# Cross-attention with layer norm: where the scale step runs, how the last keys are packed, and the order of all queues

## The chip, the cores and the metric

The kernel runs on one core of a Trainium2 chip. The time is the device time of one execution in microseconds (us); lower is better. TensorE (PE in the rows) multiplies into PSUM, VectorE (DVE), ScalarE (ACT) and GpSimd (POOL) compute elementwise, and the sync engine (SP) issues the transfers. Each engine takes its instructions in program order and waits on semaphores set by the others.

## What is computed

```python
qh = split_heads(q @ Wq.T + bq)     # q: x, 4 x 2048 x 512, 16 heads of 32
kh = split_heads(k @ Wk.T + bk)     # k, v: ctx, 4 x 77 x 512
vh = split_heads(v @ Wv.T + bv)
scores = einsum("bhqd,bhkd->bhqk", qh, kh) / sqrt(32)
scores = where(mask == 0, -1e9, scores)
m = max(scores, axis=-1, keepdims=True)
e = exp(scores - m) * mask
probs = e / (sum(e, axis=-1, keepdims=True) + 1e-9)
attn = einsum("bhqk,bhkd->bhqd", probs, vh)
x = attn @ Wo.T + bo + q
return (x - mean(x)) / sqrt(var(x) + 1e-5) * ln_g + ln_b
```

All in float32; the mask is all ones. There are 8192 query rows and 77 keys for each of 4 batches.

## The kernel before

The rows are cut into 16 blocks b of 512; four blocks belong to a batch. A matrix product of full width is done with operands split in a high and a low part (three products into one PSUM bank). For a block the steps are:

- XH and XL (ScalarE, GpSimd) split the transposed x into `xT_hi` and `xT_lo`; Q(b, c) on TensorE gives 128 of the 512 columns of the query, c = 0 to 3, in bank `proj`; QE (ScalarE) adds the bias and moves it to `QT`.
- S_round(b, j), j = 0 to 2, computes the scores of one block of 32 keys for all 16 heads: 16 small matmuls with `ident` bring in the mask as a bias, 16 more multiply `KT` by `QT`, each on a 32 x 32 tile of the array, into the four banks `ring`. The order of key blocks is `KBLOCK` = 2, 0, 1. TI (VectorE) transposes two banks at a time from `ring` into `E`, so queries lie on partitions. `E` holds 80 columns for each head and row group of a query tile, 77 of them keys.
- MX(b, h) reduces E to the row minimum (scores have a minus sign) for one half of the query groups, h = 0, 1. EX(b, h, r) are 8 exponentials on ScalarE over 77 keys each, with the row's minimum as the bias and the sum accumulated; r = 0 to 3 are the heads of a column block; these 8 are called a group below, and two of them, (h, r) and (h, r + 1), a unit. EPS adds 1e-9, RC (VectorE) inverts, NM (GpSimd, line 643) multiplies a unit by it.
- TO (VectorE) transposes back into `PT_main` (two key blocks) and `PT_tail` (the last keys, of heads r and r + 1 in the two halves of one 32 block). AV(b, h) multiplies by `V_main` and `V_tail` into `ring`, 48 matmuls of 32 x 32 tiles. Two instructions make one float32 matmul, so the rows count 96.
- AH and AL (ScalarE, VectorE) split the result, OUT(b, t) multiplies 128 rows by Wo (1 bias matmul and 12 others), t = 0 to 3. RS (VectorE) adds x, SS computes the statistics. RD (GpSimd) computes `rstd` for two t, LN (GpSimd) has three operations: centre and scale (line 667), times `ln_g`, plus `ln_b`. The sync engine stores the tile and loads the next x into the ring `Y` of 8 tiles.

K of batch 0 comes first (K_first); K_rest and V(0) to V(3) stand in pass 0 of TensorE's loop, ahead of Q(1, 0). V leaves PSUM into `V_sb`, which lies in the memory of PT, and `place_values` moves it in 24 transfers to `V_main` and `V_tail` before TO of block 0 may write. The order on each engine is written out by hand in one loop over passes; in pass m TensorE works on scores of block m, on AV of blocks m - 1 and m - 2 and on OUT of block m - 2.

## Time and profile before

| | us |
|---|---|
| median of 3 runs (lowest, highest) | 665.72 (664.99, 667.14) |
| the profiled execution's own time | 666.48 |
| its span, first to last instruction | 664.3 |
| TensorE busy | 571.9 |
| VectorE busy | 451.9 |
| ScalarE busy | 470.4 |
| GpSimd busy | 549.6 |

The span is one execution on the chip. Busy time is that of instructions at work; for TensorE the ends of pipelined matmuls are modelled. A timeline row gives start, duration, engine, line and operation, and x4 means four such instructions merged. A group row ends in busy us, mean ns of one, and the idle time before it with what released it.

### The profile page before, as it was taken

The numbers are of one execution on the slowest core, as the hardware profiler recorded it, in microseconds if no ns is written. First come the engines' busy times: TensorE is split into PE (matmuls) and PEld (weight loads), VectorE is DVE, ScalarE is ACT, GpSimd is POOL, SyncE is SP. The second block draws the span as 40 slices with busy tenths as digits, with TensorE's granted clock in tenths as the row PEclk, the third lists the DMA queues.
The fourth block names the chain that finished last, engine by engine and source line by source line (L and its number), as shares of the span: only waits on it lengthen the run. The fifth ranks groups of instructions, "written<-read, shape, count | busy, mean of one in ns | idle before, by whom it ended". The sixth has DMA issues, their size and how long they took to land.

```text
span 664.3 us, 18292 instructions
## 1 busy us (share of the span) xinstructions
PE 571.9 (86%) x7072; PEld 391.8 (59%) x7072; DVE 451.9 (68%) x607; ACT 470.4 (71%) x2315; POOL 549.6 (83%) x393
## 2 busy tenths in 40 slices
PE   6699466999998989998998999898999898969480
PEld 4455235676666657675766676666666675737350
DVE  3452317788686877786868878686778787887540
ACT  3202297798887877889795979787788787888600
POOL 0110145699999999999999999999999999999998
PEclk9889776999999999999998999998999999977695
DMA  8961241202313141404040414122231411032111
GB/s 269 238 144 32 66 149 48 65 33 85 109 61 132 35 149 43 145 33 159 34 161 28 147 36 126 68 87 106 64 129 39 153 62 56 35 111 76 53 40 56
DMA packets 35073, 60.80 MB, mean 92 GB/s; under 512 B 4957, under 2 KB 6493, under 8 KB 34988
## 3 DMA queue, kind: packets, MB, share of 16 engines
q1 hardware_dynamic: 34988, 59.66, 28.8%
q8 instruction: 55, 0.90, 0.6%
q14 instruction: 30, 0.25, 0.1%
HBM read 42.23 MB, written 16.78 MB: 89 GB/s over the span
## 4 chain that ended last, share of the span: by engine, by line
POOL 79%; PE 9%; issue 4%; SPq 3%; DVE 2%; ACT 1%; DMA 1%; POOLq 0%; ACTq 0%
POOL Y L667 20%; POOL E L643 20%; POOL Y L670 12%; POOL Y L672 12%; POOL xT_lo L636 10%; POOL rstd L657 3%; SPq L220 2%; PE proj L294 2%; PE proj L330 2%; PE proj L304 2%; DVE E L510 1%; PE ring L382 1%; DVE rowmin L517 1%; POOL var_eps L654 1%; PE ring L359 1%
## 5 line engine op out<-in xcount | busy, mean ns | idle before, releaser
L451 ACT ACTIVATE E<-E,rowmin 128x77 f32<-128x77 f32 x1024 | 352.1, 354 | 0.0
L451 ACT ACTIVATION_READ_ACCUMULATOR E<-E,rowmin 128x1 f32 x1024 | 198.8, 194 | 0.0
L643 POOL TENSOR_TENSOR E<-E,inv_sum 128x1232 f32<-128x1232 f32 x64 | 145.7, 2288 | 43.9 <-DVE inv_sum L525 43.9
L667 POOL TENSOR_SCALAR Y<-Y,mean_var,rstd 128x512 f32<-128x512 f32 x64 | 133.1, 2080 | 3.4 <-POOL rstd L657 0.2
L537 DVE STREAM_TRANSPOSE PT_main<-E 128x1024 f32<-128x1024 f32 x64 | 79.3, 1240 | 81.7 <-POOL E L643 76.4
L510 DVE STREAM_TRANSPOSE E<-ring 128x1024 f32<-128x1024 f32 x96 | 115.1, 1226 | 23.8 <-PE ring L359 23.8
L636 POOL TENSOR_TENSOR xT_lo<-xT_in,xT_hi 128x512 fp32r<-128x512 f32 x60 | 75.6, 1294 | 44.8 <-ACT xT_hi L433 44.8
L469 ACT ACTIVATE AT_hi<-ring 128x512 fp32r<-128x512 f32 x64 | 34.8, 596 | 103.8 <-PE ring L382 103.8
L517 DVE TENSOR_REDUCE rowmin<-E 128x32 f32<-128x2496 f32 x32 | 86.6, 2707 | 0.1
L670 POOL TENSOR_TENSOR Y<-Y,g_row 128x512 f32<-128x512 f32 x64 | 82.2, 1284 | 5.3
L672 POOL TENSOR_TENSOR Y<-Y,b_row 128x512 f32<-128x512 f32 x64 | 82.2, 1284 | 5.0
L382 PE MATMUL ring<-PT_main,V_main 32*32 32x256 f32 x2048 | 50.5, 408 | 39.6 <-DVE PT_tail L539 31.5
L294 PE MATMUL proj<-xT_hi,WqT_lo 128*128 128x512 f32 x240 | 72.4, 426 | 3.6 <-POOL xT_lo L636 2.8
L401 PE MATMUL proj<-WoT_hi,AT_lo 128*128 128x512 f32 x256 | 71.7, 402 | 0.0
L401 PE MATMUL proj<-WoT_lo,AT_hi 128*128 128x512 f32 x256 | 71.5, 402 | 0.0
L401 PE MATMUL proj<-WoT_hi,AT_hi 128*128 128x512 f32 x256 | 70.9, 399 | 0.0
L443 ACT ACTIVATE QT<-proj,biases 128x512 f32<-128x512 f32 x64 | 43.6, 682 | 34.4 <-PE proj L294 27.6
L359 PE MATMUL ring<-QT,KT 32*32 32x512 f32 x1536 | 67.3, 622 | 0.0
L294 PE MATMUL proj<-xT_lo,WqT_hi 128*128 128x512 f32 x240 | 66.6, 400 | 0.0
L294 PE MATMUL proj<-xT_hi,WqT_hi 128*128 128x512 f32 x240 | 64.9, 392 | 0.0
L294 PEld LDWEIGHTS proj<-xT_hi,WqT_lo 128*128 128x128 f32 x240 | 45.3, 199 | 32.6 <-issue 18.1
L558 DVE TENSOR_TENSOR Y<-proj,Y 128x512 f32<-128x512 f32 x64 | 42.8, 668 | 29.8 <-PE proj L401 29.8
(59 smaller groups left out, 745.3 us busy)
## 6 DMA issues: line engine op xcount, KB each, us to landing
xT_in<-in_xT SPq DMA_DIRECT2D x64, 256.0 KB, 3.0
Y<-in_x SPq DMA_DIRECT2D x64, 256.0 KB, 4.5
out_y<-Y SPq DMA_DIRECT2D x64, 256.0 KB, 2.0
E<-in_maskT SPq DMA_DIRECT2D x16, 192.0 KB, 11.0
Y<-in_WqT SPq DMA_DIRECT2D x4, 256.0 KB, 5.1
PT_main<-in_WkT SPq DMA_DIRECT2D x1, 1024.0 KB, 9.9
E<-in_WvT SPq DMA_DIRECT2D x1, 1024.0 KB, 15.1
Y<-in_WoT SPq DMA_DIRECT2D x1, 1024.0 KB, 17.3
```

The costliest lines, as they stand in the source:

```text
L294: last = mm(q_bank(c)[:, :], w[:, k, c * P:c * P + P], v[:, k, :], start=(n == 0 and k == 0), stop=(n == 2 and k == C - 1))
L359: last = mm(ring[DK * c:DK * c + DK, r, :], KT[DK * r:DK * r + DK, c, batch, DK * kb:DK * kb + DK], QT[DK * r:DK * r + DK, c, :], start=Fa ...
L401: last = mm(o_bank(t)[:, :], a[:, k, t * P:t * P + P], w[:, k, :], start=False, stop=(n == 2 and k == C - 1))
L451: last = cp(e, e, ACT.Exp, scale=-1.0, bias=rowmin[:, b % 2, h, r, i:i + 1], accum_out=rowsum[:, b % 2, h, r, i:i + 1])
L510: nc.vector.transpose(dst, ring[:, 2 * p:2 * p + 2, :].rearrange("p r (a q) -> p (r a) q", q=DK)) \
L517: nc.vector.tensor_reduce(out=rowmin[:, b % 2, h, :, :], in_=E_rows[b % 2][:, :, HQ * h:HQ * h + HQ, 0:SK + 1], op=ALU.min, axis=AX.X).the ...
L537: nc.vector.transpose(PT_main[:, h, 2 * p:2 * p + 2, :, :], E_rows[b % 2][:, 2 * p:2 * p + 2, rows, 0:2 * DK])
L636: tt(xT_lo[:, k, :], xT_in[:, k, :], xT_hi[:, k, :].bitcast(FP32), ALU.subtract).then_inc(x_lo, 1)
L643: tt(e, e, inv_sum[:, b % 2, h, 2 * p:2 * p + 2, :].unsqueeze(3).broadcast_to((P, 2, HQ, SK)), ALU.mult).then_inc(probs_ready, 1)
L667: nc.gpsimd.tensor_scalar(Y[:, i, :], Y[:, i, :], mean_var[:, i, 0:1], rstd[:, i:i + 1], ALU.subtract, ALU.mult).then_inc(centered, 1)
L670: tt(Y[:, i, :], Y[:, i, :], g_row[:, :], ALU.mult).then_inc(scaled, 1)
L672: tt(Y[:, i, :], Y[:, i, :], b_row[:, :], ALU.add).then_inc(normed, 1)
```

## The change

The centring and scaling step of the layer norm goes from GpSimd to ScalarE (LS), as x * rstd + shift with per-row operands; GpSimd computes the shift, minus the mean times rstd, in two small operations per pair.

The last 13 keys of two heads share one 32 block already in the scores: K is laid out with the last keys twice, each copy zero for the other head, the contraction is over 64 rows (two heads), and round 0 fills two banks with 8 mask matmuls and 8 score matmuls. TI of round 0 takes one bank at a time, 512 elements. In AV the last keys are multiplied on tiles of 32 rows and 64 columns, 8 matmuls for 16.

In the unit h = 1, r = 2 and 3 of each block the row minimum isn't a bias of the exponential: GpSimd subtracts it (SB), ScalarE takes one exponential over 16 x 77 elements (EB), VectorE adds up the rows (SM). The other three units stay as they were.

K comes out of PSUM with bias, scale and zeros in one operation by a constant loaded from the host. V is computed by 48 small matmuls per batch directly in the partitions where it is used and stored by three VectorE operations; the transfers of `place_values` go. V(0) stands in pass 0, V(1) to V(3) in passes 1 to 3 after AV, K_rest in pass 1. The host lays the context out with 96 keys per batch and the mask already spread, one transfer of it in place of four. The orders on all four compute engines are new.

```diff
+            load_mask(1)
             sp.wait_ge(mask_ready, 2)
             load_mask(2)
-            sp.wait_ge(mask_ready, 4)
-            load_mask(3)
...
-            place_values()
+            sp.wait_ge(mask_ready, 4)
+            load_mask(3)
...
-                if not has(b):
...
+                else:
                     pe.wait_ge(q_ready, 4 * (b - 1) + c + 1)
+                if b == 2:
+                    pe.wait_ge(k_ready, 2 * C)
+                if c == 3 and b <= B:
+                    pe.wait_ge(v_ready, b)
...
             def K_rest(c):
-                pe.wait_ge(q_ready, 4)
+                pe.wait_ge(q_ready, 8)
...
             def V(b):
+                if not 0 <= b < B:
+                    return
                 if b == 0:
                     pe.wait_ge(wv_loaded, 16)
-                pe.wait_ge(k_ready, C + b + 1)
-                for k in range(C):
-                    last = mm(proj[b][0:SK, :], ctxT_in[:, k, b * SK:b * SK + SK], WvT_in[:, k, :],
-                              start=(k == 0), stop=(k == C - 1))
+                    pe.wait_ge(q_ready, 4)
+                elif b == 1:
+                    pe.wait_ge(k_ready, 2 * C)
+                else:
+                    pe.wait_ge(y_ready, 4 * (b - 1))
+                for kb in range(3):
+                    for k in range(C):
+                        for c in range(C):
+                            last = mm(proj[0][DK * c:DK * c + DK, P * kb:P * kb + P],
+                                      ctxT_in[:, k, b * KP + DK * kb:b * KP + DK * kb + DK],
+                                      WvT_in[:, k, c * P:c * P + P], start=(k == 0), stop=(k == C - 1),
+                                      tile_position=(0, DK * c))
                 last.then_inc(v_ps, 1)
...
+                    for i in range(2):
+                        for c in range(C):
+                            mm(ring[DK * c:DK * c + DK, i, :], ident[2 * DK * i:2 * DK * i + DK, :],
+                               mask_bias[2 * DK * i:2 * DK * i + DK, 0, cols], start=True, stop=False,
+                               tile_position=(2 * DK * i, DK * c))
+                    for i in range(2):
+                        for c in range(C):
+                            last = mm(ring[DK * c:DK * c + DK, i, :],
+                                      KT[2 * DK * i:2 * DK * i + 2 * DK, c, batch, 2 * DK:KP],
+                                      QT[2 * DK * i:2 * DK * i + 2 * DK, c, :], start=False, stop=True,
+                                      tile_position=(2 * DK * i, DK * c))
                 else:
+                    kb = j - 1
                     pe.wait_ge(turned, 6 * b + 2 * j)
-                for r in range(R):
-                    for c in range(C):
-                        mm(ring[DK * c:DK * c + DK, r, :], ident[DK * r:DK * r + DK, :],
-                           mask_bias[DK * r:DK * r + DK, kb, cols], start=True, stop=False,
-                           tile_position=(DK * r, DK * c))
-                for r in range(R):
-                    for c in range(C):
-                        last = mm(ring[DK * c:DK * c + DK, r, :],
-                                  KT[DK * r:DK * r + DK, c, batch, DK * kb:DK * kb + DK],
-                                  QT[DK * r:DK * r + DK, c, :], start=False, stop=True,
-                                  tile_position=(DK * r, DK * c))
+                    for r in range(R):
+                        for c in range(C):
+                            mm(ring[DK * c:DK * c + DK, r, :], ident[DK * r:DK * r + DK, :],
+                               mask_bias[DK * r:DK * r + DK, j, cols], start=True, stop=False,
+                               tile_position=(DK * r, DK * c))
+                    for r in range(R):
+                        for c in range(C):
+                            last = mm(ring[DK * c:DK * c + DK, r, :],
+                                      KT[DK * r:DK * r + DK, c, batch, DK * kb:DK * kb + DK],
+                                      QT[DK * r:DK * r + DK, c, :], start=False, stop=True,
...
+                if h == 0:
+                    pe.wait_ge(v_ready, batch + 1)
                 pe.wait_ge(back_ready, 4 * b + 2 * h + 2)
                 if h == 0:
-                    pe.wait_ge(turned, 6 * min(b + 2, NB))
+                    if has(b + 1):
+                        pe.wait_ge(turned, 6 * (b + 1) + 6)
+                    elif b:
+                        pe.wait_ge(a_lo, 4 * (b - 1) + 4)
                 else:
                     pe.wait_ge(a_lo, 4 * b + 2)
-                for kb in range(3):
+                for kb in range(2):
                     for c in range(C):
                         for r in range(R):
-                            rows = slice(DK * c, DK * c + DK)
-                            v, p = ((V_main[rows, kb, batch, r, :], PT_main[rows, h, r, :, DK * kb:DK * kb + DK])
-                                    if kb < 2 else (V_tail[rows, batch, r, :], PT_tail[rows, h, r // 2, :, :]))
-                            last = mm(ring[DK * r:DK * r + DK, c, 0:HW], v, p, start=(kb == 0), stop=(kb == 2),
-                                      tile_position=(DK * c, DK * r))
+                            mm(ring[DK * r:DK * r + DK, c, 0:HW],
+                               V_main[DK * c:DK * c + DK, kb, batch, DK * r:DK * r + DK],
+                               PT_main[DK * c:DK * c + DK, h, r, :, DK * kb:DK * kb + DK],
+                               start=(kb == 0), stop=False, tile_position=(DK * c, DK * r))
+                for c in range(C):
+                    for i in range(2):
+                        last = mm(ring[2 * DK * i:2 * DK * i + 2 * DK, c, 0:HW],
+                                  V_tail[DK * c:DK * c + DK, batch, 2 * DK * i:2 * DK * i + 2 * DK],
+                                  PT_tail[DK * c:DK * c + DK, h, i, :, :], start=False, stop=True,
+                                  tile_position=(DK * c, 2 * DK * i))
                 last.then_inc(av_ps, 1)

...
             for m in range(NB + 2):
+                Q(m, 3), OUT(m - 2, 0), S_round(m, 0), OUT(m - 2, 1), S_round(m, 1), OUT(m - 2, 2), S_round(m, 2)
+                OUT(m - 2, 3)
+                if m == 0:
+                    V(0)
+                if m == 1:
+                    K_rest(0), K_rest(1), K_rest(2), K_rest(3)
+                AV(m - 1, 0), Q(m + 1, 0), Q(m + 1, 1), Q(m + 1, 2), AV(m - 1, 1)
                 if m > 0:
-                    Q(m, 2), Q(m, 3)
-                OUT(m - 2, 0), AV(m - 2, 1), OUT(m - 2, 1)
-                S_round(m, 0), OUT(m - 2, 2)
-                S_round(m, 1), OUT(m - 2, 3)
-                S_round(m, 2)
-                if m == 0:
-                    K_rest(0), K_rest(1), K_rest(2), K_rest(3), V(0), V(1), V(2), V(3)
-                    pe.wait_ge(v_ready, B)
-                Q(m + 1, 0), Q(m + 1, 1), AV(m - 1, 0)
+                    V(m)
...
+            def EB(b):
+                if not has(b):
+                    return
+                act.wait_ge(shifted, b + 1)
+                e = E_rows[b % 2][:, 2:4, HQ:QH, 0:SK]
+                cp(e, e, ACT.Exp, scale=-1.0).then_inc(unit_exp, 1)
+
             def EPS(b, h, p):
                 if not has(b):
                     return
-                act.wait_ge(exp_ready, 8 * b + 4 * h + 2 * p + 2)
+                if h and p:
+                    act.wait_ge(unit_sum, b + 1)
+                else:
+                    act.wait_ge(exp_ready, 6 * b + 4 * h + 2 * p + 2)
                 cp(rowsum_eps[:, b % 2, h, 2 * p:2 * p + 2, :], rowsum[:, b % 2, h, 2 * p:2 * p + 2, :],
                    ACT.Copy, bias=SUM_EPS).then_inc(sum_ready, 1)
+
+            def LS(b, t):
+                if not has(b):
+                    return
+                n = 4 * b + t
+                i = n % RING
+                act.wait_ge(shift_ready, 2 * b + t // 2 + 1)
+                cp(Y[:, i, :], Y[:, i, :], ACT.Identity, scale=rstd[:, i:i + 1], bias=shift[:, i:i + 1]) \
+                    .then_inc(centered, 1)

...
+            XH(1, 0), XH(1, 1), XH(1, 2), XH(1, 3)
+            for a in range(NB + 3):
+                XH(a + 1, 0) if a else None
+                EB(a - 1), EX(a - 1, 1, 0), EX(a - 1, 1, 1), EPS(a - 1, 1, 0), EPS(a - 1, 1, 1)
+                XH(a + 1, 1) if a else None
+                LS(a - 2, 0)
+                XH(a + 1, 2) if a else None
+                XH(a + 1, 3) if a else None
+                LS(a - 2, 1), AH(a - 1, 0), EX(a, 0, 0), EX(a, 0, 1), QE(a + 1, 0), LS(a - 2, 2), QE(a + 1, 1)
+                EPS(a, 0, 0), EX(a, 0, 2), QE(a + 1, 2)
...
+                AH(a - 1, 1), QE(a + 1, 3), EX(a, 0, 3), LS(a - 2, 3), EPS(a, 0, 1)
```

VectorE, GpSimd and the host's layout:

```diff
-                dst = E[:, b % 2, lo:lo + 2 * QH * PITCH].rearrange("p (n k) -> p n k", k=PITCH)[:, :, 0:DK]
-                nc.vector.transpose(dst, ring[:, 2 * p:2 * p + 2, :].rearrange("p r (a q) -> p (r a) q", q=DK)) \
-                    .then_inc(turned, 1)
+                if j == 0:
+                    dst = E_rows[b % 2][:, 2 * p:2 * p + 2, :, 2 * DK:PITCH].rearrange("p r a k -> p a r k")
+                    src = ring[:, p, :].rearrange("p (a q) -> p a q", q=DK)
+                else:
+                    dst = E_wide[b % 2][:, 2 * QH * p:2 * QH * p + 2 * QH, DK * (j - 1):DK * j]
+                    src = ring[:, 2 * p:2 * p + 2, :].rearrange("p r (a q) -> p (r a) q", q=DK)
+                nc.vector.transpose(dst, src).then_inc(turned, 1)

...
+            def SM(b):
+                if not has(b):
+                    return
+                dve.wait_ge(unit_exp, b + 1)
+                nc.vector.tensor_reduce(out=rowsum[:, b % 2, 1, 2:4, :], in_=E_rows[b % 2][:, 2:4, HQ:QH, 0:SK],
+                                        op=ALU.add, axis=AX.X).then_inc(unit_sum, 1)
+
...
+                    dve.wait_ge(bv_loaded, 16 * C)
+                tt(V_tail[:, b, :], proj[0][:, 2 * P:3 * P], bv_rows[:, :], ALU.add).then_inc(v_summed, 1)
+                tt(V_main[:, :, b, :], proj[0][:, 0:2 * P].rearrange("p (k n) -> p k n", k=2),
+                   bv_rows[:, :].unsqueeze(1).broadcast_to((P, 2, P)), ALU.add)
+                dve.wait_ge(v_summed, b + 1)
+                tt(V_tail[:, b, :], V_tail[:, b, :], value_mask, ALU.mult).then_inc(v_ready, 1)
+
             for k in range(C):
                 dve.wait_ge(wq_hi, k + 1)
                 lo(WqT_lo, WqT_in, WqT_hi, k, wq_lo)
...
+            TI(0, 0, 0), TI(0, 0, 1), TI(0, 1, 0), TI(0, 1, 1), TI(0, 2, 0)
+            for d in range(NB + 2):
+                TI(d, 2, 1)
+                if d == 0:
+                    values(0)
                 if d == 1:
+                    keys(0, False), keys(1, False), keys(2, False), keys(3, False)
                     dve.wait_ge(bo_hi, 1)
                     tt(bo_hl[DK:2 * DK, :], bo_st[DK:2 * DK, :], bo_hl[DK:2 * DK, :].bitcast(FP32),
                        ALU.subtract).then_inc(bo_lo, 1)
-                MX(d, 0), RC(d - 1, 1, 1), SS(d - 2, 3), AL(d - 1, 0), TO(d - 1, 1, 0), TO(d - 1, 1, 1)
-                MX(d, 1), RS(d - 1, 0), RC(d, 0, 0), SS(d - 1, 0), AL(d - 1, 1), RS(d - 1, 1), SS(d - 1, 1)
-                TI(d + 1, 0, 0)
+                RC(d - 1, 1, 1), MX(d, 0), SS(d - 2, 2), RS(d - 2, 3), SS(d - 2, 3), TO(d - 1, 1, 0), AL(d - 1, 0)
+                TO(d - 1, 1, 1)
+                if d == 0:
+                    masks(1), masks(2), masks(3)
+                RC(d, 0, 0), MX(d, 1), AL(d - 1, 1)
+                if d > 0:
+                    values(d)
+                TO(d, 0, 0), RS(d - 1, 0), SS(d - 1, 0), RC(d, 0, 1), TI(d + 1, 0, 0), TI(d + 1, 0, 1), SM(d)
+                RS(d - 1, 1), SS(d - 1, 1), TI(d + 1, 1, 0), TI(d + 1, 1, 1), TO(d, 0, 1), RS(d - 1, 2), RC(d, 1, 0)
+                TI(d + 1, 2, 0)

...
+            def SB(b):
+                if not has(b):
+                    return
+                pool.wait_ge(min_ready, 2 * b + 2)
+                e = E_rows[b % 2][:, 2:4, HQ:QH, 0:SK]
+                tt(e, e, rowmin[:, b % 2, 1, 2:4, :].unsqueeze(3).broadcast_to((P, 2, HQ, SK)), ALU.subtract) \
+                    .then_inc(shifted, 1)
+
...
+                tt(var_eps[:, i:i + 2], variances, ln_eps[:, :], ALU.add).then_inc(var_ready, 1)
+                tt(minus_mean[:, i:i + 2], means, minus_one[:, :], ALU.mult).then_inc(minus_ready, 1)
                 pool.wait_ge(var_ready, 2 * b + h + 1)
                 tt(rstd[:, i:i + 2], var_eps[:, i:i + 2], minus_half[:, :], ALU.pow).then_inc(rstd_ready, 1)
+                pool.wait_ge(minus_ready, 2 * b + h + 1)
+                pool.wait_ge(rstd_ready, 2 * b + h + 1)
+                tt(shift[:, i:i + 2], minus_mean[:, i:i + 2], rstd[:, i:i + 2], ALU.mult).then_inc(shift_ready, 1)
...
-                pool.wait_ge(rstd_ready, 2 * b + t // 2 + 1)
-                nc.gpsimd.tensor_scalar(Y[:, i, :], Y[:, i, :], mean_var[:, i, 0:1], rstd[:, i:i + 1],
-                                        ALU.subtract, ALU.mult).then_inc(centered, 1)
                 pool.wait_ge(centered, n + 1)
                 tt(Y[:, i, :], Y[:, i, :], g_row[:, :], ALU.mult).then_inc(scaled, 1)
                 pool.wait_ge(scaled, n + 1)
...
+            for g in range(NB + 2):
+                LN(g - 2, 0), RD(g - 2, 1), LN(g - 2, 1), LN(g - 2, 2), NM(g, 0, 0), SB(g), LN(g - 2, 3), XL(g + 2, 0)
+                NM(g, 0, 1), RD(g - 1, 0), XL(g + 2, 1), XL(g + 2, 2), XL(g + 2, 3)
+                if g == 0:
                     wo_low()
-                RD(g, 0), LN(g, 0), NM(g + 1, 0, 1), LN(g, 1), NM(g + 1, 1, 0)
+                NM(g, 1, 0), NM(g, 1, 1)

...
+    maskT = np.zeros((4, 32, 3, mask.shape[1]), mask.dtype)
+    for half in (0, 16):
+        maskT[:, half:half + tail, 0] = mask[64:]
...
+    ctxT = np.zeros((D, B, 96), ctx.dtype)
+    ctxT[:, :, 0:SK] = ctx.transpose(2, 0, 1)
+    ctxT[:, :, 80:80 + tail] = ctxT[:, :, 64:64 + tail]
+    row, half = np.arange(128), np.arange(32) // 16
+    real = np.arange(32) % 16 < tail
+    consts = np.zeros((128, 33 + 96 + 128), np.float32)
     consts[:, 0:32] = np.tile(np.eye(32, dtype=np.float32), (4, 1))
-    consts[:, 32] = np.tile(np.where(np.arange(32) < keys - 64, 1e9, 5e8), 4)
```

## Rows read from the trace of the kernel before

**Rows 1.** The page's first line.
```profile
span 664.3 us, 18292 instructions
```

**Rows 2.** Busy time by stretch, 280 to 320; columns length, PE, PEld, DVE, ACT, POOL.
```profile
280.00:320.00 40.00, 37.52 (x543) 26.29 (x544) 31.78 (x44) 31.81 (x157) 38.82 (x28) 1.00 0.27 87
```

**Rows 3.** Chain that ended last, GpSimd low halves of x; columns start, us, what.
```profile
300.56 4.99 POOL xT_lo L636 x4
...
335.82 4.99 POOL xT_lo L636 x4
```

**Rows 4.** Timeline of GpSimd; columns start, us, engine, line, operation.
```profile
318.41 4.52 POOL L643 TENSOR_TENSOR E<-E,inv_sum 128x1232 f32<-128x1232 f32 x2
322.88 0.21 POOL L654 TENSOR_TENSOR var_eps<-mean_var,ln_eps 128x2 f32<-128x2 f32 x1
...
323.98 2.08 POOL L667 TENSOR_SCALAR Y<-Y,mean_var,rstd 128x512 f32<-128x512 f32 x1
...
328.76 2.09 POOL L667 TENSOR_SCALAR Y<-Y,mean_var,rstd 128x512 f32<-128x512 f32 x1
```

**Rows 5.** Timeline of TensorE in the same block.
```profile
317.38 1.19 PE L294 MATMUL proj<-xT_hi,WqT_lo 128*128 128x512 f32 x4
...
322.99 0.40 PE L398 MATMUL proj<-bo_hl,ones 128*128 128x512 f32 x1
...
326.11 1.28 PE L382 MATMUL ring<-PT_main,V_main 32*32 32x256 f32 x50
...
328.17 0.50 PE L398 MATMUL proj<-bo_hl,ones 128*128 128x512 f32 x1
328.50 1.10 PE L401 MATMUL proj<-WoT_lo,AT_hi 128*128 128x512 f32 x4
...
331.40 0.43 PE L354 MATMUL ring<-mask_bias,ident 32*32 32x512 bf16 x16
...
332.89 0.50 PE L398 MATMUL proj<-bo_hl,ones 128*128 128x512 f32 x1
```

**Rows 6.** Groups of ScalarE: busy us, mean ns | idle before.
```profile
L451 ACT ACTIVATE E<-E,rowmin 128x77 f32<-128x77 f32 x1024 | 352.1, 354 | 0.0
...
L443 ACT ACTIVATE QT<-proj,biases 128x512 f32<-128x512 f32 x64 | 43.6, 682 | 34.4 <-PE proj L294 27.6 <-PE proj L304 6.8
```

**Rows 7.** Timeline of ScalarE, two exponentials that follow each other.
```profile
299.74 0.35 ACT L451 ACTIVATE E<-E,rowmin 128x77 f32<-128x77 f32 x1
...
300.08 0.35 ACT L451 ACTIVATE E<-E,rowmin 128x77 f32<-128x77 f32 x1
```

**Rows 8.** Groups of VectorE.
```profile
L510 DVE STREAM_TRANSPOSE E<-ring 128x1024 f32<-128x1024 f32 x96 | 115.1, 1226 | 23.8 <-PE ring L359 23.8
L517 DVE TENSOR_REDUCE rowmin<-E 128x32 f32<-128x2496 f32 x32 | 86.6, 2707 | 0.1
...
L539 DVE STREAM_TRANSPOSE PT_tail<-E 128x256 f32<-128x256 f32 x64 | 25.8, 402 | 0.0
```

**Rows 9.** Timeline of the start: TensorE, and the sync engine's queue between.
```profile
35.28 7.93 PE L321 MATMUL proj<-ctxT_in,PT_main 128*128 128x231 f32 x32
43.73 13.93 PE L330 MATMUL proj<-E,ctxT_in 128*77 128x512 f32 x32 [0.52 <-DVE KT L585]
...
63.71 14.92 SPq L220 DMA_DIRECT2D V_tail<-PT_main  x16
...
104.74 2.30 PE L382 MATMUL ring<-PT_main,V_main 32*32 32x256 f32 x60 [8.11 <-issue]
```

**Rows 10.** Timeline of TensorE at the end.
```profile
593.43 2.33 PE L382 MATMUL ring<-PT_main,V_main 32*32 32x256 f32 x61 [3.92 <-DVE PT_tail L539]
...
643.36 1.09 PE L401 MATMUL proj<-WoT_hi,AT_hi 128*128 128x512 f32 x4
```

**Rows 11.** Groups of TensorE.
```profile
L359 PE MATMUL ring<-QT,KT 32*32 32x512 f32 x1536 | 67.3, 622 | 0.0
...
L382 PE MATMUL ring<-PT_main,V_main 32*32 32x256 f32 x2048 | 50.5, 408 | 39.6 <-DVE PT_tail L539 31.5 <-issue 8.1
```

177 lines of the change are left out of this document (69 added, 108 removed).

## The prediction

> **What bounds the kernel now.** I read, in this order: the page's head, the table by stretch, the chain that ended last, the timeline of each engine over one block of 512 rows, then the start and the end. The span is 664.3 us [rows 1]; the profiled execution took 666.48 us, 2.2 more, and the median of the runs is 0.8 below that. In a middle stretch GpSimd works 38.82 of 40 us, TensorE 37.52, VectorE 31.78, ScalarE 31.81 [rows 2]. The chain runs on GpSimd without a break and repeats every 35.26 us (300.56 to 335.82) [rows 3]. So a block costs what GpSimd's list costs, and the list adds up: four normalizations of E at 2.24, four layer norms at 4.78 (323.98 to 328.76), the low halves of x 5.0, two rstd pairs at 1.10 (322.88 to 323.98): 35.3 [rows 3, 4]. The reader should see that TensorE stands close behind, which decides what the cut is worth. Its list, by starts in an unbroken stretch: a Q column block is 2.80 (317.38 to 322.99 is two), OUT 3.12 to 3.23, AV 2.06, a score round 1.49 [rows 5]. Times 4, 4, 2 and 3: 11.2 + 12.7 + 4.1 + 4.5 = 32.5.
>
> **GpSimd, part by part.** The centring (2.08 and 0.07 of wait) goes: 4 x 2.1 = 8.5 off. SB, subtracting the row minimum for one unit, has the shape of the normalization: +2.24. Each rstd pair gains two operations like the 0.21 one and a wait, about 0.45: +0.9 [rows 4]. 35.3 - 8.5 + 2.24 + 0.9 = 29.9 us a block.
>
> **ScalarE.** 16 of the 64 exponentials go, 0.34 each by their starts (299.74, 300.08) [rows 7]: -5.5. One exponential over 1232 elements comes: from 354 ns at 77 and 682 at 512 elements, 1.2 us; it can't be less than the 0.68 of 512 elements, nor more than the 5.5 it replaces. Four scale steps come at 0.75 each (from the 0.68 row; between 0.6 and 1.0): +3.0 [rows 6]. ScalarE works about 29 us a block now and 28 then. The Trainium skill, "ScalarE: Activation LUTs", section on what ACT_TABLE_LOAD costs, adds about 93 ns for each per-partition operand; by it a scale step would be 0.8 and a block 0.2 more on ScalarE, which is not the bound.
>
> **VectorE.** The first round's two transposes shrink from 1024 to 512 elements: between 402 ns (256) and 1226 (1024) [rows 8] that is 0.68 each, -1.1. SM adds a reduction of half the elements of the 2707 ns one, +1.35 [rows 8]. 28.0 a block (31.78 of 40, rows 2, times 35.26) becomes 28.2.
>
> **TensorE.** The first score round issues 8 + 8 matmuls in place of 16 + 16 (one fp32 matmul is two pieces), but each still streams 512 columns and they run side by side before too, so only the staggered start shrinks: 1.49 to between 1.2 and 1.5, I take 1.35. AV issues 80 pieces for 96; 2.06 / 96 is 21.5 ns a piece, so 1.72 at best. New here is a change of tile shape inside the round (32 rows to 64 rows) and inside each AV (32 to 64 columns). The one shape change I can price is between full and 32-wide: coming from AV, OUT's second matmul starts 0.33 after its first (328.17, 328.50) where Q's follow at 0.23 (5.61 / 24), and into AV or a round the start is some 0.1 late (OUT is 3.23 and 3.12, not 13 x 0.23) [rows 5]. I take 1.88 for AV. Sum: 11.2 + 12.7 + 1.35 + 2.98 + 3.76 = **32.0 a block**, 31.6 without any cost of shape. GpSimd's 5.3 us therefore give back only to TensorE's 32.0: the bound moves.
>
> **Does the new order let TensorE run?** I walk a block from t = 0, the last transposed round (AV of head half 0 begins, MX can begin). VectorE: MX 2.7, one residual and the statistics of two row tiles, TO, AL, TO: done at 9.4; TensorE needs that for the second AV at 1.9 + 3 x 2.8 = 10.3. ScalarE from 2.9: two groups of eight exponentials 5.5, QE, scale, QE, sum, a third group: 13.2; QE and AH: 14.8; AL 15.7; the next score round, after Q and OUT, comes at 18.2. Each round is followed by one OUT (3.2), under which two transposes (2.38) fit with 0.7 to spare; the last pair ends at about t + 31.3. GpSimd waits for the fourth scale step (18.8), then layer norm, low half, normalization, rstd: 26.5, and ScalarE wants that rstd at 27.2. Nothing exceeds 32.0, but the margins are 0.7, 0.7, 0.9: I add 0.2 of friction, **32.2**.
> New waits and what is queued behind: scale steps wait for the shift from GpSimd (behind them the copies of x and AH); layer norm waits for the scale step (behind it a normalization and all low halves); SM waits for the wide exponential (behind it the transposes that release score round 2); Q column 3 waits for V. The store and load queue keeps its order and loses the 24 placing transfers.
>
> **The start.** Before, AV of block 0 begins at 104.74: V takes 13.93 us of TensorE ahead of Q(1), and the last 16 placing transfers are issued from 63.71 for 14.92 us, until 78.6, holding PT and the loads behind them [rows 9]. After: rounds as before, first minimum at 41.5 (V of one batch under the transposes); two groups, two QE, a group, QE, the five copies of bo and Wo, QE: first round of block 1 at 55; a group, reciprocal at 58; rounds 1 and 2 to 67; K of the other batches, 288 for 231 columns, 7.93 [rows 9] to some 8.5: AV of block 0 at **75.5**. Bounds 70 and 83 (mask 3 now leaves after mask 1 was read, and holds the next loads).
>
> **V in the loop.** In blocks 1 to 3 V stands between AV and Q column 3 in one bank: TensorE reaches V at 12, finishes at 14.6, VectorE is free only at 15.6 and needs 1.0, Q resumes at 16.7 for 12.0: 3 x 4.7 = 14. Bounds 8 (if the ends overlap) and 16.
>
> **The end.** From AV of block 14 at 593.43 [rows 10] it is 70.9 to the end, with GpSimd the last engine; TensorE was done 51 after that AV (643.36 + 1.09) [rows 10]. I take 49 to 50 for TensorE, then residual and statistics 1.6, rstd 1.5, three layer norms 8.1, store 2.5: 63. Bounds 61 and 66.
>
> **Sum.** 75.5 + 14 x 32.2 + 14 + 63 = 603.3 span; + 2.2 = 605.5; 0.8 lower for the median: **605**. (The same sum before: 104.7 + 14 x 34.9 + 70.9 = 664.3.)
>
> **Rivals.** (1) TensorE stalls at each new shape: each waits until the pieces in flight (0.4 us by the 408 ns of one; 0.62 in a score round) [rows 11] are out, and a 64-column weight load takes as long as two of 32, so the 16 saved pieces save nothing: AV 2.4, round 1.9; block 33.2 to 33.7, and the VectorE margins of 0.7 are spent: 620 to 627. For it: three of them per block. Against it: the shape changes that exist cost 0.1 to 0.2 [rows 5]. The Trainium skill, "TensorEngine Tiling (Array Packing)", key properties, states that changing the tiling mode drains TensorE; that is this rival, and the rows show such a change to cost far less than a whole drain. The same time comes from ScalarE or VectorE missing a margin by a microsecond or two. 0.33.
> (2) TensorE's list is cheaper than I add (rounds and AV shrink with their instruction counts): GpSimd stays the bound at 30.3: 75.5 + 14 x 30.3 + 14 + 63 + 1.4 = 578. Against it: 23.9 us are unchanged Q and OUT. 0.06.
> (3) Slower than before: the round trip VectorE statistics, GpSimd rstd, ScalarE scale, GpSimd layer norm. Both queues are in order; if a scale step waits behind a late rstd, exponentials behind it are late, then reciprocals, then the normalizations behind which the rstd itself stands. Each such miss costs a normalization plus an rstd, 3.7. It makes the kernel slower once a block exceeds 32.2 + 60.7 / 14 = 36.5, that is more than one miss in every block: 670. My margin at that point is 0.7, but ScalarE has 3.5 idle before AH. 0.04.
> (4) The gain is eaten at the start and in V to within 0.3%: 0.01.
> My forecast (block 31.6 to 32.8, 594 to 614): 0.56.
>
> **Range.** From 588 (the gain of a free tile shape and the low bounds of start and V) to 628 (rival 1 whole). It leaves out rivals 2 to 4 and a tail of rival 1. A measurement of this kernel can tell about 0.3%. Faster 0.95, same 0.01, slower 0.04.
>
> **What would show it.** In the changed profile: GpSimd busy about 465 us and no longer the chain; TensorE the largest share of the chain; the start of AV of block b to that of b + 1 at 32.2 in the middle; AV at 1.9 and the first round at 1.35 by starts; scale steps at 0.75; AV of block 0 at 75; a gap before Q column 3 only in blocks 1 to 3. It is wrong if the period is above 33 with TensorE idle before AV or score rounds (a margin missed), or if TensorE's own list is longer (rival 1), or if ScalarE sits idle ahead of scale steps (rival 3).

## The result and the profile after

The changed kernel takes 611.95 us (median; 611.2 to 612.85), the kernel before 665.9 beside it: ratio 0.919, 95% interval 0.917 to 0.921. Forecast was 605. One of the four executions of experiment nine fell into a slower state and took 2908.8 us; the time given there is the median of the other three. The page of the changed kernel, its first lines and the shares of the chain that ended last:

```profile
span 609.9 us, 16815 instructions
## 1 busy us (share of the span) xinstructions
PE 560.1 (92%) x6528; PEld 378.3 (62%) x6528; DVE 458.3 (75%) x630; ACT 447.2 (73%) x1883; POOL 460.7 (76%) x409
...
PE 81%; ACT 8%; DVE 7%; POOL 1%; issue 1%; DMA 0%; POOLq 0%; SPq 0%; DVEq 0%
```

The same line of the page before:

```profile
POOL 79%; PE 9%; issue 4%; SPq 3%; DVE 2%; ACT 1%; DMA 1%; POOLq 0%; ACTq 0%
```

GpSimd has left the chain (79% before, 1% now), TensorE carries 81% of it. The table by stretch for 280 to 320 us (length, then PE, PEld, DVE, ACT, POOL, as in [rows 2]):

```profile
280.00:320.00 40.00, 40.00 (x454) 26.86 (x452) 34.60 (x47) 32.67 (x136) 35.18 (x34) 1.00 0.30 97
```

TensorE works 40.00 of 40 us, at full granted clock (1.00, the level of 2.4 GHz). So one block should cost exactly its list of TensorE; experiment five tests that. Here is the list by starts, the timeline of TensorE over one block (start us, busy us, engine, line, operation), the answer to [rows 5]:

```profile
287.50 1.49 PE L400 MATMUL ring<-PT_main,V_main 32*32 32x256 f32 x64
...
289.54 1.20 PE L290 MATMUL proj<-xT_hi,WqT_lo 128*128 128x512 f32 x4
...
298.14 1.49 PE L400 MATMUL ring<-PT_main,V_main 32*32 32x256 f32 x64
...
300.18 1.21 PE L290 MATMUL proj<-xT_hi,WqT_lo 128*128 128x512 f32 x4
...
303.09 0.40 PE L424 MATMUL proj<-bo_hl,ones 128*128 128x512 f32 x1
...
306.22 0.41 PE L358 MATMUL ring<-mask_bias,ident 32*32 32x512 bf16 x8
...
307.57 0.50 PE L424 MATMUL proj<-bo_hl,ones 128*128 128x512 f32 x1
...
310.79 0.43 PE L372 MATMUL ring<-mask_bias,ident 32*32 32x512 bf16 x16
...
320.24 1.49 PE L400 MATMUL ring<-PT_main,V_main 32*32 32x256 f32 x64
```

AV 2.04 (287.50 to 289.54), three Q columns 8.60 (to 298.14), AV 2.04, the fourth Q 2.91 (to 303.09), OUT 3.13, first score round 1.35 (306.22 to 307.57), OUT 3.22, round 1.50, OUT 3.23, round 1.50, OUT 3.22: **32.74** from 287.50 to 320.24. Eleven blocks in a row have this period; the first three take 37.14, 39.10 and 37.57 (AV of block 0 starts at 75.45, then 112.59, 151.69, 189.26), and the AV of block 14 starts at 549.42, 60.5 before the end.

Where the 54.4 us of span went, by the same three parts before (104.74, 14 blocks to 593.43, 70.9; [rows 9, 10]) and after: 29.3 at the start, 14.7 in the 14 blocks (488.69 became 473.97, with 15.6 us of V in it now), 10.4 at the end. Without V the 14 blocks are 30.3 shorter. No run isolates what the start gave: that V, its 24 transfers and the mask loads made it is read from [rows 9], not tested.

Two groups of the page, layer norm's first product on GpSimd and the new scale step on ScalarE (busy us, mean ns | idle before, its releaser):

```profile
L737 POOL TENSOR_TENSOR Y<-Y,g_row 128x512 f32<-128x512 f32 x64 | 82.8, 1294 | 49.5 <-ACT Y L503 49.5
...
L503 ACT ACTIVATE Y<-Y,shift,rstd 128x512 f32<-128x512 f32 x64 | 51.1, 804 | 16.1 <-POOL shift L727 16.1
```

GpSimd waits for the scale step in almost every block; ScalarE's 16.1 us are three waits in all. Both are off the chain. In the timeline of GpSimd [rows 4] it looks so:

```profile
286.62 4.52 POOL L699 TENSOR_TENSOR E<-E,inv_sum 128x1232 f32<-128x1232 f32 x2
...
302.50 2.27 POOL L707 TENSOR_TENSOR E<-E,rowmin 128x1232 f32<-128x1232 f32 x1
307.50 1.30 POOL L737 TENSOR_TENSOR Y<-Y,g_row 128x512 f32<-128x512 f32 x1 [2.73 <-ACT Y L503]
...
315.62 3.80 POOL L692 TENSOR_TENSOR xT_lo<-xT_in,xT_hi 128x512 fp32r<-128x512 f32 x3 [0.67 <-ACT xT_hi L458]
319.37 4.51 POOL L699 TENSOR_TENSOR E<-E,inv_sum 128x1232 f32<-128x1232 f32 x2
```

From one pair of normalizations to the next, 286.62 to 319.37, it is 32.75, of which 3.40 are the two waits in brackets, 2.73 for a scale step and 0.67 for a copy of x: 29.35 of work.

### The profile page after: what moved, and what is told of

Same layout as the page of the kernel before. It is cut to its first block, busy times and chain, and to the rows that moved or that the text cites. A ratio compares the mean times of both kernels' runs of the same rounds, so it can differ in the third digit from the quotient of the medians.

```text
span 609.9 us, 16815 instructions
## 1 busy us (share of the span) xinstructions
PE 560.1 (92%) x6528; PEld 378.3 (62%) x6528; DVE 458.3 (75%) x630; ACT 447.2 (73%) x1883; POOL 460.7 (76%) x409
## 4 chain that ended last, share of the span: by engine, by line
PE 81%; ACT 8%; DVE 7%; POOL 1%; issue 1%; DMA 0%; POOLq 0%; SPq 0%; DVEq 0%
PE proj L427 29%; PE proj L290 23%; PE ring L400 6%; PE ring L377 6%; ACT E L476 6%; PE proj L424 4%; PE ring L406 3%; PE ring L363 3%; PE proj L300 2%; PE ring L372 2%; PE proj L317 2%; DVE E L554 1%; DVE rowmin L560 1%; ACT QT L468 1%; DVE AT_lo L599 1%
## 5 line engine op out<-in xcount | busy, mean ns | idle before, releaser
L476 ACT ACTIVATE E<-E,rowmin 128x77 f32<-128x77 f32 x768 | 263.8, 350 | 18.7 <-DVE rowmin L560 18.7
L476 ACT ACTIVATION_READ_ACCUMULATOR E<-E,rowmin 128x1 f32 x768 | 146.3, 191 | 0.0
L554 DVE STREAM_TRANSPOSE E<-ring 128x1024 f32<-128x1024 f32 (+1 forms) x96 | 95.9, 1037 | 9.6 <-PE ring L377 6.2
L290 PE MATMUL proj<-xT_hi,WqT_lo 128*128 128x512 f32 x240 | 69.2, 410 | 5.7 <-DVE V_tail L649 5.7
L427 PE MATMUL proj<-WoT_hi,AT_lo 128*128 128x512 f32 x256 | 70.3, 396 | 0.0
L503 ACT ACTIVATE Y<-Y,shift,rstd 128x512 f32<-128x512 f32 x64 | 51.1, 804 | 16.1 <-POOL shift L727 16.1
L290 PEld LDWEIGHTS proj<-xT_hi,WqT_lo 128*128 128x128 f32 x240 | 43.0, 188 | 24.6 <-issue 16.2
L427 PEld LDWEIGHTS proj<-WoT_hi,AT_lo 128*128 128x128 f32 x256 | 48.3, 189 | 11.9
## 6 DMA issues: line engine op xcount, KB each, us to landing
WvT_in<-in_WvT SPq DMA_DIRECT2D x1, 1024.0 KB, 10.4
```

The source lines that it names most:

```text
L290: last = mm(q_bank(c)[:, :], w[:, k, c * P:c * P + P], v[:, k, :], start=(n == 0 and k == 0), stop=(n == 2 and k == C - 1))
L427: last = mm(o_bank(t)[:, :], a[:, k, t * P:t * P + P], w[:, k, :], start=False, stop=(n == 2 and k == C - 1))
L476: last = cp(e, e, ACT.Exp, scale=-1.0, bias=rowmin[:, b % 2, h, r, i:i + 1], accum_out=rowsum[:, b % 2, h, r, i:i + 1])
L503: cp(Y[:, i, :], Y[:, i, :], ACT.Identity, scale=rstd[:, i:i + 1], bias=shift[:, i:i + 1]) \
L554: nc.vector.transpose(dst, src).then_inc(turned, 1)
```

## The experiments

The code cuts are abridged: `...` marks lines that are left out, and indices, flags and unchanged waits are shortened.

**One, was it the centring on GpSimd?** LS goes and with it the two small shift operations, LN centres again; all orders stay.

```
 def LS(b, t):
+    return
...
 def LN(b, t):
+    pool.wait_ge(rstd_ready, ...)
+    nc.gpsimd.tensor_scalar(Y, Y, mean_var, rstd, ALU.subtract, ALU.mult)
```

> The changed kernel with the centring and scaling step of the layer norm back on GpSimd (ScalarE's scale steps and the two small shift operations gone), every order kept. Theory, the bound moved from GpSimd to TensorE and comes back with this step: GpSimd is busy 28.6 us a block in the changed kernel (87% of 32.74); + 4 x 2.16 - 0.34 = 36.9, so a block of 36.9 with no gap on GpSimd, TensorE idle some 4 us a block, 665 to 680 us in all. Rival, the new orders and the shorter TensorE work carry the steady gain: a block stays under 34, below 640 us.

Measured: 678.25 us, ratio to the kernel before 1.019 (1.017 to 1.021); AV of head half 0 at 299.05 and 336.32, so 37.3 a block. The table by stretch shows GpSimd at 39.16 of 40:

```profile
280.00:320.00 40.00, 37.02 (x411) 23.65 (x410) 27.24 (x37) 26.48 (x121) 39.16 (x27) 0.96 0.26 85
```

GpSimd bounds this kernel, and the scale step is what lifts it: without it the rest of the change takes 1.9% longer than the kernel before, since SB's 2.3 us a block stay on GpSimd. Undoing this one part costs 66 us, more than the change gave.

**Two, is the scale step enough?** The kernel before, its orders and its exponentials, with only the scale step moved to ScalarE (put in where ScalarE's list has room).

```
+def LS(b, t):
+    act.wait_ge(shift_ready, ...)
+    cp(Y, Y, ACT.Identity, scale=rstd, bias=shift)
...
-EX(a, 0, 3), EX(a, 1, 0), EPS(a, 0, 1), EX(a, 1, 1)
+EX(a, 0, 3), EX(a, 1, 0), EPS(a, 0, 1), EX(a, 1, 1), LS(a - 1, 0)
...
```

> The kernel before with one part of the change alone: the layer norm's scale step on ScalarE and the shift on GpSimd, all other orders kept; the four scale steps stand where GpSimd has the rstd ready (two ahead of AH of the second half, two after the third and sixth group of exponentials of the pass). Theory, the step frees GpSimd (35.3 - 8.6 + 0.45 = 27 us a block) and the bound becomes TensorE's 32.6 or ScalarE's list (29 + 3 = 32 to 32.5) with some waits between them: 33 to 34 a block, the start at 104.7 as before, 640 to 652 us. So it would give half or less of the change's 54 us, and the rest belongs to the start and the shorter lists. Rival, the order written for the old lists doesn't carry it, ScalarE and GpSimd wait for each other around the scale step: 35 or more a block, 660 us or more.

Measured: 674.61 us, ratio 1.012 (1.010 to 1.014): 1.2% longer, small but clear of the noise. Blocks alternate between 35.1 and 36.6. The view of waits (who waited for whom: us in total, times, longest) and the timeline of GpSimd:

```profile
POOL Y L688 <- ACT Y L474: 134.4, 32, 6.9
...
DVE PT_main L552 <- POOL E L658: 68.8, 17, 8.6
```

```profile
308.98 0.20 POOL L678 TENSOR_TENSOR shift<-minus_mean,rstd 128x2 f32<-128x2 f32 x1
313.14 1.30 POOL L688 TENSOR_TENSOR Y<-Y,g_row 128x512 f32<-128x512 f32 x1 [3.96 <-ACT Y L474]
```

and ScalarE between the two:

```profile
308.71 0.36 ACT L457 ACTIVATE E<-E,rowmin 128x77 f32<-128x77 f32 x1
...
312.24 0.82 ACT L474 ACTIVATE Y<-Y,shift,rstd 128x512 f32<-128x512 f32 x1
```

The shift is ready at 309.2; ScalarE works through its exponentials until 312.24 before it comes to the scale step, and GpSimd, emptied of 8.5 us a block, idles for such steps 134 us in all, some 8.4 a block. The chain that ended last passes through this step: scale step 312.35, layer norm 313.14, normalization 315.80, transposes back 318.07, AV 319.69, after it Q and the second AV, AH 334.62, exponentials, the next scale step 348.93. That is a ring of 36.6 us. The outcome is that of the prediction's third rival (slower), by another path: no rstd is late, the scale step stands behind exponentials. It holds for my placing of the steps in the old order; another placing may do better and wasn't tried. Taken alone and so placed, the move brings nothing.

**Three, what is the fourth unit without row bias worth?** The last unit gets its 16 exponentials with row bias again; SB, EB and SM go.

```
-EB(a - 1), EX(a - 1, 1, 0), EX(a - 1, 1, 1), EPS(a - 1, 1, 0), EPS(a - 1, 1, 1)
+EX(a - 1, 1, 0), EX(a - 1, 1, 1), EPS(a - 1, 1, 0), EX(a - 1, 1, 2), EX(a - 1, 1, 3), EPS(a - 1, 1, 1)
```

> The changed kernel with the fourth unit again as 16 exponentials with row bias and accumulated sum; the subtraction on GpSimd, the wide exponential and the row sum on VectorE are gone. Theory, ScalarE had room: it sits idle 4.46 us a block ahead of AH and gets 5.5 - 1.24 = 4.3 us more; TensorE stays the bound at 32.7 to 33.0 a block, 612 to 617 us. Rival, this part was needed: ScalarE becomes the bound, its copies of x and scale steps come 4.3 us later, GpSimd's low halves and the normalization behind them too, VectorE waits for these: 34 or more a block, 630 us or more.

Measured: 644.88 us, ratio 0.969 (0.966 to 0.973). The theory (ScalarE had room) failed and the rival was right, by 33 us over the changed kernel. The table by stretch and the chain of this run (start, us, what):

```profile
280.00:320.00 40.00, 38.13 (x475) 25.61 (x444) 29.60 (x39) 37.16 (x171) 31.63 (x29) 1.00 0.26 87
```

```profile
301.29 0.61 ACT xT_hi L458
...
301.97 3.75 POOL xT_lo L689 x3
305.72 4.47 POOL E L696 x2
310.19 1.27 POOL Y L734
...
314.15 0.02 ACT Y L500
...
324.58 5.49 ACT E L476 x32
...
330.09 0.22 ACT rowsum_eps L491
330.31 5.50 ACT E L476 x32
...
335.97 0.61 ACT xT_hi L458
```

The first three blocks take 39.1, 40.8 and 41.3, the later ones 35.0 on average (34.4 to 36.2). The chain is a ring of 34.7 us (301.29 to 335.97) in which neither engine is full: ScalarE works 37.16 of 40, GpSimd 31.63. Exponentials, copy of x, low half, normalization, layer norm, rstd, scale step, exponentials. The unit without row bias takes 4.2 us (16 x 0.34 less 1.24) out of ScalarE's leg of this ring and costs GpSimd 2.3 and VectorE 1.4, where there was room. I had counted busy time, and not the ring.

**Four, the shape of the tail of AV.** 16 products of 32 x 32 instead of 8 of 32 x 64, so that AV has 96 pieces again and no change of shape.

```
-for i in range(2):
-    mm(ring[64*i:64*i+64, c, 0:HW], V_tail[..., 64*i:64*i+64], PT_tail[..., h, i], ...)
+for r in range(R):
+    mm(ring[32*r:32*r+32, c, 0:HW], V_tail[..., 32*r:32*r+32], PT_tail[..., h, r // 2], ...)
```

> The changed kernel with the last keys of AV multiplied by 16 matmuls on 32 x 32 tiles, as before, in place of 8 on 32 x 64. Theory, a shape change of the array inside AV eats what the 16 saved pieces give: AV by starts was 2.06 before and is 2.04 now, so it comes to 2.04 to 2.08 and the time to 611.5 to 613.5. Rival, the saved pieces are worth 21.5 ns each and something else makes AV long in the changed kernel: AV 2.35, 0.6 us a block, 620 us. Rival on the other side, without a shape change AV is shorter: below 2.0 and below 611.

Measured: 612.35 us, ratio 0.919 (0.917 to 0.920), and the AV stage of the trace 2.06 us for 2.04. The same. The 16 saved pieces would be 0.34 us at the 21.5 ns a piece that the prediction took. The starts of single matmuls in the two traces show where they went. In the changed kernel the first 64-wide piece starts 0.30 us after the last 32-wide one, in each of the 22 AVs between 150 and 500 us; the longest step inside an AV of one shape is 0.19. The 16 wide pieces then take 0.31 us from the first start to the last, 20 ns each, where the 96 narrow ones take 18. So a wide piece costs little more than a narrow one, and most of what the 16 saved pieces give is lost in the step between the shapes. Of that 0.30 at least 0.11 is the change itself; the two runs don't tell more. The row after such a change:

```profile
288.92 0.69 PE L406 MATMUL ring<-PT_tail,V_tail 32*64 32x256 f32 x16
```

The Trainium skill, "TensorEngine Tiling (Array Packing)", key properties, has TensorE drain at such a change. The trace agrees in that the step is longest there, 0.30 us; whether all pieces in flight are out by then it can't tell, since the ends of matmuls are modelled.

**Five, is TensorE's list the only bound in the middle?** The product that adds bo in OUT is taken out (the output lacks bo).

```
-mm(o_bank(t)[:, :], ones[:, :], bo_hl[:, :], start=True, stop=False)
```

> The changed kernel without the matmul that adds bo in OUT, so the output lacks bo: 4 matmuls of 128 x 512 less a block, 0.24 us each by their starts. Theory, TensorE's list is the whole bound: a block of 32.74 - 0.96 = 31.8, TensorE without a gap, 595 to 599 us. Rival, the margins of VectorE and ScalarE (0.7 us by the walk of the prediction) are used up on the way: a block of 32.2 or more, TensorE waits for the turned scores or for AH and AL, 603 us or more.

Measured: 601.23 us; AV at 285.80 and 317.62, a block of 31.82. All of the 0.92 us is passed on, with no wait of TensorE in that stretch, so the other engines still had 0.9 us of room. The whole is 2 us above the expectation, because AV of block 0 comes at 76.7 for 75.45 and the first three blocks take 36.2, 38.5 and 38.9, together only 0.2 less than in the changed kernel. TensorE waits 6.6 us for V's sums there, for 5.7 in the changed kernel: the multiplications of V_tail in blocks 2 and 3 take 1.45 and 1.93 us for 1.08 and 1.09, since they fall differently beside GpSimd (last section). The rest of the 2 us stays open.

**Six and seven, does a product's step hang on where its operands lie?** By starts, a Q product in the changed kernel takes 0.2334 us and before 0.2292, with the same instruction. The change moved the buffers. 32 or 96 empty bytes a partition go ahead of xT_in:

```
+pad = sb("pad", [P, 8], FP32)
 xT_in = sb("xT_in", [P, C, ROWS], FP32)
```

> The changed kernel with an unused buffer of 32 bytes a partition ahead of the x buffers. It is to explain why the unchanged Q matmuls follow each other at 0.233 us in the changed kernel (289.54 to 298.14 for 36, shape change included) and at 0.229 before. The smaller constants and bias rows moved the moving operand xT_hi in the program's layout from byte 77760 (a multiple of 64, not of 128) to 77152 (32 past a multiple of 64); with this pad it starts at 77184, a multiple of 128. Theory, the start address decides and a multiple of 64 is enough: Q at 0.229, 0.22 us a block less, 608 to 609.5 us. Rival, a multiple of 128 is as slow (OUT, whose moving operand Wo starts at a multiple of 128, takes 0.233 in both kernels): 611 to 613 us, and the pad of 96 is faster than this one. Second rival, the bank or the order of the steps decides: no change in either pad.

> As the run before with a pad of 96 bytes: xT_hi starts at 77248, a multiple of 64 but not of 128, as in the kernel before. Theory and first rival alike: Q at 0.229 and 608 to 609.5 us. Second rival, the address has no part in it: 0.233 and 611 to 613 us.

Measured: 605.65 us (ratio 0.908, 0.907 to 0.909) with 32 bytes, 610.39 (0.915, 0.913 to 0.916) with 96. Unused bytes bring 6.3 us. Both expectations missed: 32 bytes gave more than the 608 to 609.5 of the theory, 96 bytes less, though its Q step did fall to that of the kernel before. I read it so that a multiple of 128 was fast, and tested this in two more kernels: all of ones, bo_hl, x and A at multiples of 128 (64 bytes ahead of ones, 96 ahead of xT_in, together with the change of experiment nine), and 64 bytes ahead of xT_in in the kernel before.

> The run before with 64 empty bytes a partition ahead of ones and 96 ahead of xT_in, so that ones, bo_hl, xT_hi, xT_lo, AT_hi and AT_lo all begin at a multiple of 128 bytes. Theory: the step of TensorE's 128x512 products hangs on the start address of the operands; with all at multiples of 128 a product takes 0.2266 us in Q and OUT alike. A Q column is then 2.72 to 2.76 us instead of 2.87, an OUT column 3.04 to 3.08 instead of 3.12, the block 32.74 - 4 x 0.12 - 4 x 0.06 = 32.0 us, and the kernel 7 to 10 us under the run before (588 to 591 us). Rival: the stationary operand or the row of ones is what counts in OUT, and only Q gains, as with the pad of 32 bytes: block 32.27, 5 to 6 us under the run before.

> The kernel before with 64 empty bytes a partition ahead of xT_in, so that xT_hi, xT_lo, AT_hi and AT_lo begin at a multiple of 128 bytes instead of 64 past one. Theory: the product's step falls from 0.2288 to 0.2266 us, which takes 96 x 0.0022 = 0.2 us off TensorE's 32.5 us of work a block, and nothing off the period of 35.26 us, since GpSimd bounds it: 664 to 667 us. Rival: TensorE bounds enough of the period (start, end and the ring through the layer norm) for its gain to be passed on: 662 us or less.

Both missed on the step. The full alignment gives 598.70 us, only 1.2 under its partner of experiment nine (block 32.64 for 32.73) and far from both of its expectations; the kernel before gives 665.51, ratio 0.999 (0.998 to 1.000), which is no change as expected, but its step didn't fall either. The steps side by side (the rest is what remains of the start byte of xT_hi when it is divided by 256; AT_hi has the same rest in every kernel; start bytes by adding up the buffers in the order of the code, in units of 32 bytes, from the bytes that the first of these expectations names; steps are the mean distance of the starts of neighbouring products between 150 and 500 us, at most 0.3 us apart; the expectations name 0.2266 for the fast step, which is lower than this count gives):

| kernel | rest of the start byte by 256 | Q step, us | OUT step, us |
|---|---|---|---|
| 32 bytes (e5) | 128 | 0.2280 | 0.2286 |
| 96 bytes (e6) | 192 | 0.2293 | 0.2330 |
| before | 192 | 0.2292 | 0.2330 |
| full alignment (e10) | 0 | 0.2323 | 0.2323 |
| before, 64 bytes (e11) | 0 | 0.2327 | 0.2325 |
| after | 96 | 0.2334 | 0.2330 |

The steps account for the blocks: 48 Q and 48 OUT products at 0.0054 and 0.0044 us less are 0.47, and the block is 32.27 with 32 bytes for 32.74. Only a rest of 128 is fast in both; 192 comes near it in Q and gains nothing in OUT. The last run was made to tell the address from the order of work: the 32 bytes in the order of experiment nine.

> V of batches 1 to 3 in the idle time of pass 1, and 32 empty bytes a partition ahead of xT_in: xT_hi then begins at byte 77184 and AT_hi at 163200, both 128 past a multiple of 256. So far the Q product's step was 0.2266 us with xT_hi 128 past a multiple of 256, 0.2287 to 0.2297 with 192 past, 0.2306 to 0.2330 with 0 past, and 0.2335 with 96 past. Theory: the address decides, and a multiple of 128 is not enough, it must be an odd one (the weights are at odd ones too); then the step is 0.2266 us in this order as well, the block 32.27 us, and the kernel 12 to 14 x 0.47 = 5.6 to 6.6 us under the version with V in the idle time alone: 594 to 595 us. Rival: the step of 0.2266 us belongs to the order of work in the run with the 32 bytes (who else reads the memory beside TensorE), not to the address: then the step is about 0.231 us as with the full alignment, the block 32.6, and the kernel at 598 to 600 us.

Measured: 593.66 us, ratio 0.891 (0.890 to 0.893), Q step 0.2278, OUT step 0.2294, all 14 blocks between 32.28 and 32.29, and 6.3 us under experiment nine. The address theory as reworded holds in a second order of work, and this is the fastest kernel of the study. Its Q products, in the timeline of TensorE, follow at 0.91 for four, where the changed kernel's follow at 0.93 to 0.94:

```profile
309.68 1.07 PE L291 MATMUL proj<-xT_hi,WqT_lo 128*128 128x512 f32 x4
310.59 1.07 PE L291 MATMUL proj<-xT_lo,WqT_hi 128*128 128x512 f32 x4
```

Open is why. The weights lie at a rest of 128 in all kernels, and all buffers behind a pad move with it, so whether it is the rest itself, its match with the weights, or another buffer's place was not separated.

**Eight, V's place in the loop.** V before the second AV, and its sums ahead of AL on VectorE.

```
-AV(m - 1, 0), Q(m + 1, 0), Q(m + 1, 1), Q(m + 1, 2), AV(m - 1, 1)
+AV(m - 1, 0), Q(m + 1, 0), Q(m + 1, 1), Q(m + 1, 2)
 if m > 0:
     V(m)
+AV(m - 1, 1)
```

> The changed kernel with V(m) ahead of the second AV on TensorE and its three VectorE operations ahead of AL, so that VectorE has moved V before TensorE wants the bank for Q column 3. In the changed kernel blocks 1 to 3 take 37.14, 39.10 and 37.57 us from AV to AV against 32.74 later, 15.6 us more. Theory, the work of V (2.1 to 2.8 us each on TensorE) must stay, the waits for VectorE (1.6 to 2.0 us) and the clock drop in the second of them go: blocks of 35.2 to 35.8, 7 to 8 us less in all, 604 to 606 us. Rival, the rest is a wait elsewhere (x's low halves or the shifted scale steps in the first blocks): less than 3 us, 609 us or more.

Measured: 605.97 us, ratio 0.908 (0.906 to 0.910); blocks 36.67, 35.49, 35.49, then 32.74. In the changed kernel the wait stands here (timeline of TensorE), and VectorE explains it (its own timeline):

```profile
88.13 2.83 PE L334 MATMUL proj<-WvT_in,ctxT_in 128*32 128x128 f32 x96
92.57 1.17 PE L290 MATMUL proj<-xT_hi,WqT_lo 128*128 128x512 f32 x4 [1.62 <-DVE V_tail L649]
```

```profile
90.41 1.29 DVE L599 TENSOR_TENSOR AT_lo<-ring,AT_hi 128x512 fp32r<-128x512 f32 x2 [0.93 <-ACT AT_hi L513]
91.61 0.28 DVE L645 TENSOR_TENSOR V_tail<-proj,bv_rows 128x128 f32<-128x128 f32 x1
```

V is done at 91.0, the sums start at 91.61 behind AL, and Q column 3 waits for the bank. With V ahead of the second AV this wait is gone in two of the three blocks; in the first 1.1 us of it stays, since the multiplication of V_tail takes 2.05 us beside GpSimd (last section). The 2.8 us of V stay in all three.

**Nine, V in the idle time.** V of batches 1 to 3 around the first score round of block 1, where TensorE stands still, each into a bank of its own.

```
 Q(m, 3), OUT(m - 2, 0)
+if m == 1: V(1), V(2)
 S_round(m, 0)
+if m == 1: V(3)
...
-if m > 0: V(m)
```

> The changed kernel with V of the other three batches taken out of the ends of passes 1 to 3 and put into pass 1, ahead of and behind the first score round, where TensorE stood idle for 5.58, 1.92 and 2.47 us (48 to 66 us). Each V goes into a bank of its own. Theory: V in the loop lengthens blocks 1 to 3 by 4.4, 6.4 and 4.8 us (15.6 us in all: 2.83 us of V and 1.6 to 3 us of waiting for its sums on VectorE) only because of where it stands; in the idle time it costs little. AV of block 0 then starts at 75.5 to 78 us, all blocks are 32.7 to 33.2 us, and the kernel is at 596 to 600 us. Rival: the first blocks are long because of other work of the start (masks, GpSimd's low part of WoT, the loads of x), and V only lay in their idle time: then blocks 1 to 3 stay above 35 us and the kernel at 604 us or more. Second rival: the V of pass 1 pushes the whole start back by its 8.5 us, and half of the gain is lost (604 to 606 us).

Measured: 599.94 us, ratio 0.901 (0.899 to 0.903). All blocks are 32.73 from the first on, and AV of block 0 starts at 78.95: 15.6 won and 3.5 paid. The idle time that it fills, in the changed kernel, and what is in it now:

```profile
53.76 0.63 PE L358 MATMUL ring<-mask_bias,ident 32*32 32x512 bf16 x8 [5.58 <-ACT QT L468]
```

```profile
47.97 5.45 PE L333 MATMUL proj<-WvT_in,ctxT_in 128*32 128x128 f32 x192
53.65 0.41 PE L357 MATMUL ring<-mask_bias,ident 32*32 32x512 bf16 x8 [0.23 <-ACT QT L471]
55.01 2.83 PE L333 MATMUL proj<-WvT_in,ctxT_in 128*32 128x128 f32 x96
62.16 0.66 PE L371 MATMUL ring<-mask_bias,ident 32*32 32x512 bf16 x16 [4.33 <-DVE E L557]
```

V of batches 1 and 2 costs nothing. The round after V of batch 3 comes at 62.16 instead of 58.19: TensorE is done with V at 57.8 and waits for VectorE's transposes of round 0. VectorE in this run:

```profile
56.79 0.23 DVE L648 TENSOR_TENSOR V_tail<-proj,bv_rows 128x128 f32<-128x128 f32 x1
...
57.26 1.35 DVE L652 TENSOR_TENSOR V_tail<-V_tail,const_sb 128x128 f32<-128x128 f32 x1
...
59.06 1.82 DVE L652 TENSOR_TENSOR V_tail<-V_tail,const_sb 128x128 f32<-128x128 f32 x1
60.80 1.30 DVE L557 STREAM_TRANSPOSE E<-ring 128x512 f32<-128x512 f32 x2
...
62.54 0.27 DVE L652 TENSOR_TENSOR V_tail<-V_tail,const_sb 128x128 f32<-128x128 f32 x1
```

The sums of two batches hold the transposes from 56.79 to 60.80; in the changed kernel they start at 56.90. Of that 3.9, 3.5 reach AV of block 0, and 2.6 are in two multiplications that take 1.35 and 1.82 instead of 0.27 (last section).

## Why the prediction came out as it did

The forecast's mechanism held: GpSimd leaves the bound, TensorE's own list takes it, the start gives as much as the shorter blocks together (29.3 and 30.3 before V's 15.6). It was 7 us low, inside its range. Step by step:

- **GpSimd.** 29.9 us of work a block was forecast, 29.35 measured. It was right that this side of the sum doesn't matter beyond TensorE's list; experiment one shows that it would have without the scale step.
- **TensorE's list, the term that was mis-sized.** 32.0 plus 0.2 of friction was forecast, 32.74 came. There was no friction at all (TensorE 40.00 of 40). Of the 0.75 by which the list is longer, 0.32 are the two AVs: "I take 1.88" stood between 1.72 and 2.06, and 2.04 came; experiment four shows that the 64-wide tail gives nothing. 0.31 are the four Q columns, 11.51 for 11.2, of which 0.2 are the step of 0.2334 for 0.2292 us: the prediction took the unchanged instructions at their old price and didn't ask where the operands lie now (experiments six and seven). 0.1 is OUT, 12.80 for 12.7. The score rounds were right: 1.35 and 1.50.
- **The walk.** No margin was missed in a middle block, and one is to be seen: it said that the last pair of transposes under an OUT leaves 0.7; in the timeline of VectorE it starts at 317.12 and takes 2.38, so ends at 319.50, and AV starts at 320.24. It also said that GpSimd would wait for a scale step, and that wait does no harm: 2.73 in a block.
- **ScalarE.** 28 was forecast; 32.67 x 32.74 / 40 is 26.7. The prediction started from 29 a block, where [rows 2] give 31.81 x 35.26 / 40 = 28.0; from there its own terms give 26.7. The scale step is 804 ns; "0.75" was from the 0.68 row, and the 0.8 that the Trainium skill, "ScalarE: Activation LUTs", section on what ACT_TABLE_LOAD costs, led to was the better figure. The trace agrees with it; off the bound it changes nothing. The exponential over 1232 elements took 1240 ns for 1.2.
- **VectorE.** 28.2 forecast, 34.60 x 32.74 / 40 is 28.3.
- **The start.** 75.5 forecast, 75.45, and so close by luck. The first round of block 1 comes at 53.76 for 55 and the rounds end at 65.90 for 67, while K of the other batches takes 9.55 for 8.5: 7.93 x 288 / 231 would have been 9.9. Two misses of 1.1 cancel.
- **V in the loop.** 14 forecast, 15.6 (4.4, 6.4 and 4.8 over 32.74); the mechanism, V behind AV and its sums behind AL, is the one that the traces show: 2.83 of V and 1.62, 2.03 and 2.04 of waiting. The other 1.6 in the second block is the clock, which the forecast had not: behind that wait Q column 3 takes 4.41 us for 2.91, with a granted clock of 0.83 from 125 to 135.
- **The end.** 63 forecast, 60.5; the lower bound was 61. The last matmul ends 47.2 after AV of block 14, where 49 to 50 was taken: most of the miss. The three last layer norms run on GpSimd at 1.26 an operation without waits between them, 7.7 for 8.1.
- **Together:** 603.3, and 14 x 0.54 = 7.6 for the blocks, 1.6 for V, 2.5 off at the end: 610.0, with 609.9 in the trace.
- **The first rival** was half right: the 16 saved pieces bring nothing in the sum, since TensorE steps by 0.30 us at the change to the 64-wide tail, where this rival gave a stall 0.4. But a wide piece is nearly as cheap as a narrow one, so AV is 2.04 and not 2.4. The forecast's 1.88 gave the change 0.16 too little. The first score round got its 0.14. **The third** was priced at 0.04 for the whole change, and there it didn't come; with the orders of before its outcome comes, through exponentials ahead of the scale step and not through a late rstd (experiment two), and with the exponentials of before its ring, rstd, scale step, exponentials and normalization, takes 33 us (experiment three).

## What to carry to other kernels

When an operation is moved from the bound engine to one with room, add up the ring it closes and not the busy time: the scale step takes 66 us off within the new orders, and adds 8 alone in the old ones. When the bound moves to TensorE, its list by starts is the block time (32.74 both here); then each change of tile shape must be priced as a change, and the unchanged products must be priced again if buffers moved. Work that is needed once goes into the idle time of the start, into free banks, and what follows from it on another engine must not stand ahead of what the next stage waits for.

## What the runs showed of the hardware

Where the operands lie changes the step of a 128x512 Q product from 0.2280 to 0.2334 us, 2.4%, with nothing else changed: 32 unused bytes a partition took 6.3 us off in one order of work (611.95 to 605.65) and 6.3 in another (599.94 to 593.66). Fast was a rest of 128 by 256 bytes; 192, 0 and 96 gave blocks of 32.57, 32.64 and 32.74 for 32.27.

Across a change from 32 to 64 columns of tile within a stage the next piece starts 0.30 us later, for at most 0.19 inside one shape, which eats what the 16 saved pieces are worth (AV 2.04 for 2.06 us), while the change from 32 to 64 rows in the first score round left a gain of 0.14 (1.35 for 1.49).

A multiplication on VectorE with both operands in SBUF waits out GpSimd. The 128x128 one of V_tail takes 0.27 to 0.28 us where GpSimd stands idle (62.54 in experiment nine), but 1.35 and 1.82 us beside these, whose ends (58.46, 60.74) decide its own (58.61, 60.88):

```profile
57.18 1.28 POOL L699 TENSOR_TENSOR xT_lo<-xT_in,xT_hi 128x512 fp32r<-128x512 f32 x1 [3.95 <-ACT xT_hi L461]
58.42 2.32 POOL L706 TENSOR_TENSOR E<-E,inv_sum 128x1232 f32<-128x1232 f32 x1
```

In the changed kernel it takes 1.08 us at 128.90 and ends at 129.98, beside a subtraction on GpSimd that ends at 129.84. The sum just before it, with one operand in PSUM, keeps its 0.28 us in the same company (58.53). The Trainium skill, "SBUF — State Buffer", section on the two separate sides, says of the port pair that VectorE and GpSimd share that the first to start of a VectorE operation with two SBUF inputs and a GpSimd operation that reads SBUF holds it for its whole length, and the other blocks. The trace agrees: GpSimd had started first each time (57.18, 58.42), and the multiplications end 0.15 us after it.
